# An adaLN block on one Trainium2 core: the MLP activation's square and its low part move from GpSimd to VectorE

## The reference, cut to what matters

```python
h = layernorm(x) * (1 + ca) + sa
x = x + ga * attention(h)             # windowed attention, plus attention over 256 routed rows
h = layernorm(x) * (1 + cb) + sb
hid = square(relu(h @ W_fc.T))        # 512 x 1024
y = hid @ W_proj.T
spikes = 5 steps of: reset = (mem - 1 > 0); mem = 0.9 * mem + y - reset; spike = (mem - 1 > 0)
x = x + gb * spikes.mean()
```

## Time and profile before

| | |
|---|---|
| device time, median of 3 runs | 951.44 us (949.25 to 951.9) |
| profiled execution: time, span | 952.84 us, 951.1 us |
| PE busy | 838.1 us (88%), 8914 matmuls |
| DVE busy | 594.4 us (62%), 1602 instructions |
| ACT busy | 587.5 us (62%), 1682 instructions |
| POOL busy | 393.6 us (41%), 436 instructions |
| chain that ended last | PE 64%, DVE 18%, ACT 6%, issue 5%, POOL 3% |
| mean granted TensorE clock | 0.954 |

### The profile page before, as it was taken

One profiled execution on the slowest core, in us unless ns is written; L12 is line 12 of the kernel. 1 busy time (PEld: TensorE's weight loads), 2 busy tenths in 40 slices (PEclk: granted clock), 3 DMA queues, 4 the chain that ended last, 5 costly groups with the idle time before them and its releaser, 6 DMA issues.

```text
span 951.1 us, 23414 instructions
## 1 busy us (share of the span) xinstructions
PE 838.1 (88%) x8914; PEld 632.1 (66%) x8914; DVE 594.4 (62%) x1602; ACT 587.5 (62%) x1682; POOL 393.6 (41%) x436
## 2 busy tenths in 40 slices
PE   4769689989998999999998999998998999899775
PEld 2437457667776777677766777677766777678574
DVE  6746644776568747785668746785668746523544
ACT  1157566676567765676567766776567665677332
POOL 3410231346342753356342843366332833233533
PEclk7969779999999999999999999999999999999878
DMA  8220012200120012200130002200130002100100
GB/s 309 69 78 30 27 36 68 62 2 18 51 94 32 7 35 90 63 2 18 51 101 24 13 29 90 63 2 24 46 101 24 13 29 68 51 2 13 46 5 23
DMA packets 32480, 45.33 MB, mean 48 GB/s; under 512 B 3929, under 2 KB 26721, under 8 KB 32369
## 3 DMA queue, kind: packets, MB, share of 16 engines
q1 hardware_dynamic: 26944, 31.24, 10.1%
q0 software_dynamic: 4608, 12.59, 4.0%
q10 hardware_dynamic: 816, 0.00, 0.0%
HBM read 28.85 MB, written 14.97 MB: 46 GB/s over the span
## 4 chain that ended last, share of the span: by engine, by line
PE 64%; DVE 18%; ACT 6%; issue 5%; POOL 3%; DMA 2%; another core or an unknown queue 1%; SPq 1%; DVEq 0%; POOLq 0%; ACTq 0%
PE ps_unit L986 24%; PE ps_y L1098 7%; PE ps_unit L1035 6%; PE ps_turned L1149 5%; PE ps_scores L1123 4%; PE ps_turned L1184 4%; PE ps_unit L1040 3%; PE ps_turned L1169 3%; PE ps_scores L1132 3%; ACT probs L920 2%; DVE late L1335 2%; DVE routed L1308 2%; DVE late L1334 2%; DVE row_min L1412 2%; DVE late L1332 1%
## 5 line engine op out<-in xcount | busy, mean ns | idle before, releaser
L920 ACT ACTIVATE probs<-ps_scores,row_min 128x192 f32<-128x192 f32 (+2 forms) x384 | 161.5, 426 | 131.7 <-DVE row_min L1412 88.1
L930 ACT ACTIVATE probs<-probs,row_inv 128x192 f32<-128x192 f32 (+2 forms) x384 | 155.5, 456 | 0.4 <-DVE row_inv L1422 0.4
L1412 DVE TENSOR_REDUCE row_min<-ps_scores 128x2 f32<-128x512 f32 (+1 forms) x128 | 78.8, 615 | 85.2 <-PE ps_scores L1132 54.4
L986 PE MATMUL ps_unit<-xT,wqkv 128*128 128x512 f32 x384 | 112.2, 430 | 13.6 <-POOL xT L740 13.6
L512 POOL TENSOR_TENSOR hid<-hid 128x512 f32<-128x512 f32 (+1 forms) x64 | 63.6, 994 | 129.0 <-ACT hid L898 127.9
L1149 PEld LDWEIGHTS ps_turned<-ident,probs 64*128 64x128 f32 x1280 | 56.9, 140 | 84.5 <-issue 79.6
L1098 PE MATMUL ps_y<-wprojT,hid_parts 128*128 128x256 f32 x768 | 106.4, 287 | 1.4 <-POOL hid_parts L516 0.8
L1149 PE MATMUL ps_turned<-ident,probs 64*128 64x64 f32 x1280 | 82.2, 239 | 27.2 <-DVE loT L1429 24.5
L1098 PEld LDWEIGHTS ps_y<-wprojT,hid_parts 128*128 128x128 f32 x768 | 98.5, 191 | 6.8 <-issue 3.0
L986 PEld LDWEIGHTS ps_unit<-xT,wqkv 128*128 128x128 f32 x384 | 72.0, 197 | 42.6 <-issue 28.7
L986 PE MATMUL ps_unit<-h_parts,wfcT 128*128 128x512 f32 x336 | 92.6, 411 | 7.2 <-ACT full L855 5.0
(11 more groups left out here) (167 smaller groups left out, 1726.0 us busy)
## 6 DMA issues: line engine op xcount, KB each, us to landing
xa<-in_L_attn_x SPq DMA_DIRECT2D x8, 512.0 KB, 4.6
routed<-sorted_rows SPq DMA_DIRECT2D x16, 256.0 KB, 2.9
lx<-in_L_attn_x SPq DMA_DIRECT2D x8, 512.0 KB
out_x<-spikes SPq DMA_DIRECT2D x16, 256.0 KB, 2.2
routed_out<-late SPq DMA_DIRECT2D x8, 256.0 KB, 2.1
full<-mod_rows SPq DMA_DIRECT2D x7, 256.0 KB, 4.3
sorted_rows<-hn,rank POOLq DMA_INDIRECT x64
gate_a<-mod_rows SPq DMA_DIRECT2D x8, 128.0 KB
```

The costliest lines, as they stand in the source:

```text
L920: ins = act.activation(probs[:, probs_buffer(n), probs_columns(s, part)], ps_scores[:, part, lo:hi], ACT.Exp, bias=row_min[:, n % 3, part: ...
L930: ins = act.activation(rows, rows, ACT.Identity, scale=row_inv[:, n % 3, part:part + 1])
L986: ins = pe.matmul(ps, w(wi, k, w_cols), a(ai, k, a_cols), start=(n == 0), stop=(n == 3 * KD - 1))
L1412: ins = dve.tensor_reduce(row_min[:, n % 3, :], ps_scores[:, :, lo:hi], AX.X, ALU.min)
```

## The change

In the loop and last batches the square and the subtraction leave GpSimd. VectorE gets two new kinds of unit. FS i waits for the Relu (new semaphore relu_made) and makes hid_square = max(ps, 0) * hid_relu with one scalar_tensor_tensor that reads the FC product from PSUM and the Relu from SBUF; it is FS that frees the PSUM bank now. FD i subtracts the high part from hid_square. FS i stands at the end of its chunk's slot, FD i at the head of the units of the next slot (FD 4 of the last batch in slot 14 and so on). ScalarE's Relu no longer frees the bank; its Square waits for the Relu alone. TensorE does nothing for FS and FD. The tail keeps its division between GpSimd and VectorE; there square_low only counts its squares in another way.

```diff
--- before.py
+++ after.py
@@ -66,15 +66,15 @@
     7: [("HV", 1)],
     8: [("HV", 0)],
     9: [("Z3", 0), ("HQ", 0), ("Z3", 1)],
-    10: [("HK", 0), ("FC", 0)],
-    11: [("FC", 1), ("SR", 0)],
-    12: [("YA", 0), ("FC", 2), ("YA", 1)],
-    13: [("FC", 3)],
-    14: [("FC", 4), ("RK", 0), ("YA", 2), ("SR", 1), ("YA", 3)],
-    15: [("FC", 5)],
-    16: [("FC", 6), ("YA", 4), ("HQ", 1)],
-    17: [("ZT", 0), ("YA", 5), ("HK", 1), ("FC", 7)],
-    18: [("RK", 1), ("YA", 6), ("ZT", 1)],
+    10: [("HK", 0), ("FC", 0), ("FS", 0)],
+    11: [("FD", 0), ("FC", 1), ("SR", 0), ("FS", 1)],
+    12: [("FD", 1), ("YA", 0), ("FC", 2), ("YA", 1), ("FS", 2)],
+    13: [("FD", 2), ("FC", 3), ("FS", 3)],
+    14: [("FD", 3), ("FC", 4), ("RK", 0), ("YA", 2), ("SR", 1), ("YA", 3), ("FS", 4)],
+    15: [("FD", 4), ("FC", 5), ("FS", 5)],
+    16: [("FD", 5), ("FC", 6), ("YA", 4), ("HQ", 1), ("FS", 6)],
+    17: [("FD", 6), ("ZT", 0), ("YA", 5), ("HK", 1), ("FC", 7), ("FS", 7)],
+    18: [("FD", 7), ("RK", 1), ("YA", 6), ("ZT", 1)],
     19: [("NK", 0), ("YA", 7)],
     20: [("NQ", 0), ("NV", 0), ("NV", 1)],
     21: [("LO", 0), ("NV", 2)],
@@ -94,16 +94,16 @@
     6: [("HK", 1)],
     7: [("HV", 0)],
     8: [("Z3", 0), ("Z3", 1)],
-    9: [("FC", 0), ("Q", 2)],
-    10: [("FC", 1), ("K", 2)],
-    11: [("FC", 2), ("YA", 0)],
-    12: [("FC", 3), ("YA", 1)],
-    13: [("Q", 3), ("FC", 4), ("YA", 2)],
-    14: [("K", 3)],
-    15: [("FC", 5), ("YA", 3)],
-    16: [("FC", 6), ("YA", 4)],
-    17: [("FC", 7), ("YA", 5)],
-    18: [("HX", 0), ("HX", 1)],
+    9: [("FC", 0), ("Q", 2), ("FS", 0)],
+    10: [("FD", 0), ("FC", 1), ("K", 2), ("FS", 1)],
+    11: [("FD", 1), ("FC", 2), ("YA", 0), ("FS", 2)],
+    12: [("FD", 2), ("FC", 3), ("YA", 1), ("FS", 3)],
+    13: [("FD", 3), ("Q", 3), ("FC", 4), ("YA", 2), ("FS", 4)],
+    14: [("FD", 4), ("K", 3)],
+    15: [("FC", 5), ("YA", 3), ("FS", 5)],
+    16: [("FD", 5), ("FC", 6), ("YA", 4), ("FS", 6)],
+    17: [("FD", 6), ("FC", 7), ("YA", 5), ("FS", 7)],
+    18: [("FD", 7), ("HX", 0), ("HX", 1)],
     19: [("YA", 6), ("YA", 7)],
     20: [("LX", 0)],
     22: [("LX", 1)],
@@ -145,7 +145,7 @@
 FIRST_UNITS = {8: [("WF", 0)], 9: [("WF", 1)], 10: [("WF", 2)], 11: [("WF", 3), ("WP", 0)], 12: [("WP", 1)],
                13: [("WP", 2), ("WP", 3)]}
 FIRST_WEIGHTS = [u for units in FIRST_UNITS.values() for u in units]
-EARLIER_UNITS = [(k, i) for k in ("HO", "Z3", "FC", "YA") for i in range(FT)] + [("LO", T - 1)]
+EARLIER_UNITS = [(k, i) for k in ("HO", "Z3", "FC", "FS", "FD", "YA") for i in range(FT)] + [("LO", T - 1)]
 
 
 PROJECTED_AHEAD = [("NQ", 1), ("NV", 0), ("NV", 1), ("NV", 2)]
@@ -181,7 +181,8 @@
             + [u for i in range(3, 2 * FT) for u in (("FC", i), ("YA", i - 2))]
             + [("YA", 2 * FT - 2), ("YA", 2 * FT - 1)],
 }
-BANKED = {s: [u for u in units if u[0] != "YA"] for s, units in SEGMENTS.items()}
+UNBANKED = ("FS", "FD", "YA")
+BANKED = {s: [u for u in units if u[0] not in UNBANKED] for s, units in SEGMENTS.items()}
 USES = {s: [len(u[k::BANKS]) for k in range(BANKS)] for s, u in BANKED.items()}
 
 
@@ -446,6 +447,7 @@
         h2_high = sem("h2_high")
         h2_low = sem("h2_low")
         hid_squared = sem("hid_squared")
+        relu_made = sem("relu_made")
         hid_high = sem("hid_high")
         hid_low = sem("hid_low")
         tail_squared = sem("tail_squared")
@@ -496,22 +498,20 @@
         def x2_rows(n):
             return x2_last if n == B - 1 else x2
 
-        def square_low(eng, segment, b, i):
-
-            _, cols = chunk_tokens(segment, i)
-            low, count = low_made_of(segment, b, i)
-            squared, square = (hid_squared, hid_square[:, cols]) if low is hid_low else \
-                (tail_squared, hid_square[:, N // 2:N])
-            if segment == "tail" and i % 2 == 0:
-                square = hid_square[:, 0:N // 2]
-            wait_drained(eng, segment, b, ("FC", i))
-            if segment == "tail" and i == 1:
+        def square_low(eng, b, i):
+
+            _, cols = chunk_tokens("tail", i)
+            low, count = low_made_of("tail", b, i)
+            squared, times = (tail_squared if i % 2 else hid_squared), i // 2 + 1
+            square = hid_square[:, N // 2:N] if i % 2 else hid_square[:, 0:N // 2]
+            wait_drained(eng, "tail", b, ("FC", i))
+            if i == 1:
                 eng.wait_ge(hid_low, FT * (B - 1))
-            elif segment == "tail" or i > 0:
+            else:
                 eng.wait_ge(low, count - 1)
             eng.tensor_tensor(square, hid_relu[:, i % 2, cols], hid_relu[:, i % 2, cols],
                               ALU.mult).then_inc(squared, 1)
-            eng.wait_ge(squared, count)
+            eng.wait_ge(squared, times)
             eng.wait_ge(hid_high, FT * (b - 1) + i + 1)
             eng.tensor_tensor(hid_parts[1][:, i % 2, cols], square, hid_parts[0][:, i % 2, cols].bitcast(F32),
                               ALU.subtract).then_inc(low, 1)
@@ -752,8 +752,8 @@
             def unit(segment, b, u):
                 kind, i = u
                 if kind == "FC":
-                    if segment != "tail" or i % 2 == 0:
-                        square_low(pool, segment, b, i)
+                    if segment == "tail" and i % 2 == 0:
+                        square_low(pool, b, i)
                 elif kind == "ZT":
                     low_part(segment, b, i)
                 elif kind in ("LO", "LX"):
@@ -895,8 +895,12 @@
                     elif segment in ("last", "tail"):
                         act.wait_ge(hid_low, n - 1)
                     _, cols = chunk_tokens(segment, i)
-                    act.activation(hid_relu[:, i % 2, cols], ps[:, cols], ACT.Relu).then_inc(free, 1)
-                    wait_drained(act, segment, b, u)
+                    if segment == "tail":
+                        act.activation(hid_relu[:, i % 2, cols], ps[:, cols], ACT.Relu).then_inc(free, 1)
+                        wait_drained(act, segment, b, u)
+                    else:
+                        act.activation(hid_relu[:, i % 2, :], ps[:, :], ACT.Relu).then_inc(relu_made, 1)
+                        act.wait_ge(relu_made, n + 1)
                     if i >= 2 or segment == "tail" or segment == "last":
                         act.wait_ge(hid_used, n - 1)
                     act.activation(hid_parts[0][:, i % 2, cols], hid_relu[:, i % 2, cols],
@@ -991,6 +995,7 @@
                 kind, i = u
                 if kind == "YA":
                     project(segment, b, i)
+                if kind in UNBANKED:
                     return
                 if segment == "first" and u in (("HV", 0), ("HV", 1)):
                     pe.wait_ge(low_made, LOW_PARTS)
@@ -1469,6 +1474,18 @@
                     dve.tensor_tensor(ho[:, i, :], ps[:, 0:D], gate_a[:, :], ALU.mult).then_inc(free, 1)
                 elif kind in ("ZT", "Z3"):
                     high_part(segment, b, u)
+                elif kind == "FS":
+                    dve.wait_ge(relu_made, FT * (b - 1) + i + 1)
+                    ps, free = drain(segment, b, ("FC", i))
+                    if i > 0:
+                        dve.wait_ge(hid_low, FT * (b - 1) + i)
+                    dve.scalar_tensor_tensor(out=hid_square, in0=ps[:, :], scalar=0.0, in1=hid_relu[:, i % 2, :],
+                                             op0=ALU.max, op1=ALU.mult).then_inc(free, 1)
+                elif kind == "FD":
+                    wait_drained(dve, segment, b, ("FC", i))
+                    dve.wait_ge(hid_high, FT * (b - 1) + i + 1)
+                    dve.tensor_tensor(hid_parts[1][:, i % 2, :], hid_square, hid_parts[0][:, i % 2, :].bitcast(F32),
+                                      ALU.subtract).then_inc(hid_low, 1)
 
             def routed_weights(k):
 
@@ -1606,13 +1623,13 @@
             for i in range(KD):
                 high_part("tail", B, ("Z3", i))
             for i in range(1, FT, 2):
-                square_low(dve, "tail", B, i)
+                square_low(dve, B, i)
                 if i == 1:
                     third_norm(B - 1, 1)
                     for j in range(KD, 2 * KD):
                         high_part("tail", B, ("Z3", j))
             for s in range(1, STEPS):
-                square_low(dve, "tail", B, FT + 2 * s - 1)
+                square_low(dve, B, FT + 2 * s - 1)
                 neuron(B, 0, s)
             neuron(B, 0, STEPS)
             for s in range(1, STEPS + 1):
```

## The result

The changed kernel takes 958.92 us (median of 4 runs, 957.67 to 959.32), the one before 951.08 us beside it (949.25 to 951.9): ratio 1.0083, 95% interval 1.0065 to 1.0101. It is slower by 7.8 us; the forecast was 957.4. The profiled execution of after took 957.67 us, its span 955.9 us.

The account below looks back on a forecast made before the run. It took TensorE's in-order list as the main bound, with VectorE and TensorE alternately last in slots 10 to 17. Slot-by-slot terms gave +1.0 us for each of six loop batches, added to 951.44: 957.4 us, range 953 to 961.5.

Parts of the forecast that it names:

- wait ahead of FS 0: Slot 10: VectorE idles 2.06 us until the Relu of chunk 0, with statistics and router stages queued behind.
- The relief: Slots 10, 14 and 16: VectorE no longer held up while GpSimd works on SBUF; about 8 us of VectorE per batch.
- The 0.40 us at YA 3: TensorE's wait for GpSimd's low part, removed by the change; 6 x 0.40 = 2.4 us.
- level: Rival: same sum with the pause absorbed and no contention, +0.1 to +0.5 a batch; 953.5 us, chance 0.19.
- faster rival: TensorE's middle-slot waits overlap better, VectorE's ring alone bounds slots 11 to 16; -1 a batch, 945 us, chance 0.21.
- bank's wait ahead of SR 1: Slot 14: SR 1 reuses FC 4's PSUM bank, so TensorE stops there until FS 4.
- ring: Slots after 10: minimum, two exps, Relu, FS, row stage in turn; VectorE waits some 0.55 us a slot.
- wait for FD 1 ahead of YA 1: Slot 12: FD 1 ends at 420.3, so TensorE starts YA 1 at 420.35; turn of slot 12 +1.5 us.
- batches 107.1 us apart: Sign that the forecast is right: loop batches spaced 107.1 us, where the kernel before has 106.1.
- pause at the first scatter: VectorE's 1.28 us idle after the first indirect DMA; moves to SR 1 and YA 3, still paid; absorption allowed -0.9 to 0.
- contention of FD: FD 1, with two SBUF inputs, may be held up behind a GpSimd row norm; 0 to +0.55 us a batch.
- much slower rival: Subtractions delayed by the ring hold the YA that follow, waits add; +3 a batch, 969 us, chance 0.10.

Follow-up runs that it names:

- filled: The changed kernel with seven useless matmuls more per loop batch, just ahead of TensorE's wait for the router scores; 957.69 us, ratio 1.0080 to before.
- after_again: The changed kernel, unchanged, run and traced again on another chip beside the kernel before; 958.09 us, ratio 1.0102.
- relief: The kernel before with GpSimd's square and subtraction of loop and last batches cut to one column, low part left out; 915.38 us, ratio 0.9810.
- fs0_last: The changed kernel with FS 0 of the loop batches moved behind the statistics and router products of slot 10; 929.25 us, ratio 0.9958 to before.
- relu_frees: The changed kernel, but the Relu frees the PSUM bank and FS, in its old place, squares the Relu from SBUF; 939.82 us, ratio 1.0068 to before.
- deferred_2: The changed kernel with the Relu freeing the bank, FS reading SBUF, one slot later ahead of its FD; repeat on another chip; 941.53 us, ratio 0.9900.
- thin: The changed kernel with FS and FD of loop and last batches one column wide, low part left out; 947.36 us, ratio 0.9971 to before.
- before_again: The kernel before, unchanged, run and traced again on the chip of after_again; 949.18 us.

## Why the prediction was right, point by point

The forecast (957.4, slower) held, and the measured time lies 1.5 us above it. Batch 3 started at 373.68 us in before and at 373.06 in after, so times within the batch compare after adding 0.62 to those of after. Its steps:

| step | forecast against before | measured | |
|---|---|---|---|
| wait ahead of FS 0 | 2.06 | 1.96 | right |
| slot 10, router products' end | +0.76 | 413.81 + 0.62 - 413.61 = +0.82 | right |
| slot 11, products beside the row norms | +0.3 in all | one of 0.61, 0.2 | right |
| FD 1 ends | 420.3 | 419.55 + 0.62 = 420.2 | right |
| YA 1 starts | 420.35, after a wait for FD 1 | 420.8, no wait | wrong cause |
| turn of slot 12 | +1.5 | +2.05 (filled, after_again batch 2: +1.6) | half clock missed |
| turn of slot 14 | 432.4 | 432.36 + 0.62 = 433.0 | late by 0.6, carried on |
| slot 14 to 15 | 3.5 | 3.14 | pause mostly covered |
| turn of slot 15 | +1.95 | +2.18 | two misses, nearly even |
| end of the compares, slot 16 | +1.0 | 443.46 + 0.62 - 442.84 = +1.24 | right to 0.2 |
| slot 17 on | +1.05 | +1.25 (after_again batch 2: +0.86) | right to 0.2 |

**The relief** was put at 8 us of VectorE a batch, from batch 0's clean rows. The four norms took 1.53 us (forecast 1.4, before 4.87), no router product over 0.43 but one, the compares 3.02 us (440.44 to 443.46) as forecast. What it is worth in time the prediction never priced by itself; relief shows 2.9 us a batch. The 0.40 us at YA 3, put at six times, stands against GpSimd in two loop batches of six in before (3 and 4), but no term of the sum hangs on it. The level and the faster rival lived on the relief, and were wrong because FS's waits spend it, in the places where it was earned: slot 10 first.

**The waits.** The one in slot 10 was named as the first cost, and fs0_last confirms it: 2.05 us of slot 10 a batch. The bank's wait ahead of SR 1 was named, and is there at 0.66 us; relu_frees takes it away. The ring was put at some 0.55 us of VectorE's waiting in each later slot; batch 3 shows 0.54, 1.39, 0.48, 0.57, 0.65 and 0.30 us ahead of FS 1 to FS 6, the 1.39 where FC 2 itself was late. (The 2.95 us of the faster rival's ring is 2.86 by its own parts, and 2.86 in slot 14, 427.35 to 430.21; no forecast hangs on the difference.) The wait for FD 1 ahead of YA 1 was named, and is to be seen in after's batch 1 alone, and in three batches of after_again, in each case those where the clock held. The step that failed is here: the sum kept TensorE's pieces at their length behind an idle time that the change had made longer. The half clock stretched them (YA 0 2.07 us for 1.67), which made the turn of slot 12 later than the sum by 0.55 us (0.45 by the half clock, since filled is at +1.6); filled shows the forecast wait of 0.65 us as soon as the clock holds. The forecast's +1.0 a batch is what batches without the half clock show (+0.86); five with it make the sum over the six loop batches +8.7 us (636.8 to 645.6) instead of +6. Of that 8.3 lie in slots 10 to 17: 0.9 in each batch, and some 3 us for the five stretches of half clock together. The sign "batches 107.1 us apart" came out at 106.9 to 107.8 us from slot 0 to slot 0 in batches 1 to 5, over 105.6 to 106.0 in before; the 106.1 of the prediction held a slot 0 to 10 of batch 6 that was 0.9 us longer than in batches 2 to 5.

**The pause at the first scatter.** It was said to fall into SR 1 and YA 3 and to be paid all the same. The first indirect DMA did move forward:

```profile
429.89 1.13 POOL L704 DMA_INDIRECT sorted_rows<-hn,rank  x1 [9.99 <-DVE rank L1461]
```

That is 1.56 us ahead of 431.45, by this batch's clock 0.94, so it was near 430 as forecast. But the pause didn't fall where I put it: slot 13 to 14 takes 7.86 to 7.92 us in after and in fs0_last, whose chip shows no pause. It came later, at slot 15's scores, which started at 433.07 and released VectorE only at 434.34, 4.45 us behind the start of the first indirect DMA. There it costs after some 0.3 us (slot 14 to 15: 3.14, against 2.85 in fs0_last), where deferred_2 pays 1.4 (4.27 against 2.85). What before pays of its 3.47 isn't shown, since before has no trace on a chip without the pause; at most 0.6. So "paid all the same" was wrong in its place and in part in its size: the forecast had 3.5 us for slot 14 to 15, and the 0.35 too many there hid most of what the half clock had added. That these DMAs cause the pause is inferred from the times alone, here and in the prediction; no run takes them away.

**The contention of FD.** The Trainium skill ("GPSIMD Engine Reference", section 8, Key points) would expose FD, with its two SBUF inputs, to GpSimd's remaining work, and the forecast allowed FD 1 up to 0.55 us for it. FD 1 ran beside the row norms of GpSimd (416.86 to 419.89) and took 0.70 us, and all 56 have a mean of 683 ns, as undisturbed as FS with its input in PSUM (692). But the contention is there, and GpSimd pays it: the row norm beside FD 1 took 0.98 us in each of the six loop batches, and 0.47 to 0.48 in thin, where FD is one column wide. So the trace agrees with the page, and the prediction's bound for FD 1 had the wrong engine waiting. Of the work that GpSimd kept, the row norms held one router product up by 0.2 us (0.61 for 0.41).

**The rest of the program.** 0 us was put for batch 0, the last batch and the tail. In the pair of profiles batch 0 was 3.0 us shorter and the last with the tail 0.7, so that the span grew by 4.8 and not by 8.7 us. Between before and before_again, the same kernel, batch 0 differs by 2.4 us too, and in the second pair it is 1.5 us shorter in after_again; whether any of this is the change's work stays open. So that the forecast met the time within 1.5 us is in part luck: 2.7 us too few in the loop batches, and nothing put for a rest that came out shorter.

The chances: slower had 0.56. The much slower rival (+3 a batch) was nearer than it had looked: it needed the turn of slot 12 at 422.5, and it came at 421.71 + 0.62 = 422.3. Slots 14 to 17 gave back 1.28 us of that: 0.33 in slot 14 to 15, and 0.95 in slot 16 to 17 (7.28 to 6.33), where the compares are no longer held up.

## What to carry to other kernels

When work moves to an engine with a fixed order, price its place before its length: look at what the new instruction waits for, and who waits for the instructions behind it. Here 0.69 us of work a batch in front of a critical stage cost 12 us in all, by its wait and not its length; with every square one slot later, where its inputs are old, all of the added work together cost 5.8 us. And where a change lengthens TensorE's idle time, allow for a stretch at half clock behind it, which is cheap only as far as another wait covers it.
